# Graph network kernel: 127-partition gathers and a separate gather for the last partition in one sum stage

## What is computed

```python
def _hypergraph_conv(x, node_idx, edge_idx, D_inv, B_inv, W, b):
    xt = x @ W
    e = B_inv[:, None] * jax.ops.segment_sum(xt[node_idx], edge_idx, num_segments=NUM_HYPEREDGES)
    out = D_inv[:, None] * jax.ops.segment_sum(e[edge_idx], node_idx, num_segments=NUM_NODES)
    return out + b
...
h = jax.nn.relu(_hypergraph_conv(x, node_idx, edge_idx, D_inv, B_inv, W1, b1))
y = _hypergraph_conv(h, node_idx, edge_idx, D_inv, B_inv, W2, b2)
```

## Time and profile before

| | us |
|---|---|
| Median of 3 runs | 21875.0 |
| Lowest, highest | 21866.0, 21877.35 |
| Profiled execution, span from first to last instruction | 16599.4 |
| Profiled execution, its own total | not given apart from its span |
| POOL busy in the span | 11914.9 |
| DVE busy in the span | 10015.7 |
| The stage "conv1s", first gather to the end of the last | 2077.0 |

### The profile page before, as it was taken

How to read it: one execution, slowest core, us unless ns; L and a number is a source line. 1 busy time by engine, 2 the same in 40 slices (tenths; PEclk the granted TensorE clock), 3 DMA queues, 4 the chain that set the end, 5 groups by cost and what they waited for, 6 DMA issues and landing times. The chain is left out here.

```text
span 16599.4 us, 101583 instructions
## 1 busy us (share of the span) xinstructions
PE 4027.8 (24%) x22758; PEld 3127.6 (19%) x22758; DVE 10015.7 (60%) x17532; ACT 4595.6 (28%) x4609; POOL 11914.9 (72%) x12292
## 2 busy tenths in 40 slices
PE   2333356667311111111111222222111111100000
PEld 1222246666311000000000122222100000000000
DVE  7777787777573333322222477777566666576776
ACT  1111122222102222223333255554011111244342
POOL 6777757777627777767777677776777776777775
PEclk7555578888755555555555555555555555555555
DMA  2222222222262222212222234433233332344443
GB/s 85 64 60 59 59 79 80 77 78 80 102 241 55 59 59 64 60 50 64 59 60 59 74 125 133 133 125 112 63 84 84 84 84 73 118 150 156 154 152 103
DMA packets 564633, 1517.57 MB, mean 91 GB/s; under 512 B 270008, under 2 KB 270541, under 8 KB 516610
## 3 DMA queue, kind: packets, MB, share of 16 engines
q1 hardware_dynamic: 169982, 1028.88, 16.6%
q0 software_dynamic: 392160, 467.91, 12.9%
q10 hardware_dynamic: 2068, 16.12, 0.2%
HBM read 714.46 MB, written 803.57 MB: 91 GB/s over the span
## 5 line engine op out<-in xcount | busy, mean ns | idle before, releaser
L926 POOL DMA_INDIRECT rows<-tab,idx x6656 | 6444.0, 968 | 2118.2 <-issue 2027.2
L572 POOL DMA_INDIRECT moved_rows<-recs,sidx x1664 | 1687.3, 1014 | 570.7 <-issue 506.3
L926 POOL DMA_INDIRECT rows<-in_x,idx x1664 | 1588.4, 955 | 512.8 <-issue 506.8
L926 POOL DMA_INDIRECT rows<-sums,idx x1664 | 1570.2, 944 | 511.8 <-issue 506.8
L1351 DVE TENSOR_TENSOR_SCAN FB<-mask,FB 128x1430 f32<-128x1430 f32 x156 | 463.7, 3027 | 1837.1 <-ACT FB L1324 1837.1
L989 PE MATMUL dist_ps<-dist_w,a3T 65*128 65x512 f32 x416 | 392.7, 1100 | 3937.5 <-ACT a3T L1013 3920.7
L989 PEld LDWEIGHTS dist_ps<-dist_w,a3T 65*128 65x128 f32 x416 | 122.1, 324 | 4078.3 <-issue 3882.8
L1049 DVE TENSOR_REDUCE small<-SQ 128x16 f32<-128x1024 f32 x104 | 127.5, 1226 | 1083.4 <-ACT SQ L1032 726.9
L1773 PE MATMUL lg<-bd_fcr,attrT 128*128 128x128 f32 x1664 | 401.3, 422 | 1529.4 <-ACT attrT L1793 1529.4
L1324 ACT ACTIVATE FB<-rows 128x4096 f32<-128x4096 f32 x52 | 371.2, 7138 | 1349.3 <-DMA rows<-tab,idx 755.0
L1773 PEld LDWEIGHTS lg<-bd_fcr,attrT 128*128 128x128 f32 x1664 | 361.4, 321 | 1572.9 <-ACT attrT L1793 1572.8
(11 more groups left out here) (462 smaller groups left out, 19370.0 us busy)
## 6 DMA issues: line engine op xcount, KB each, us to landing
rows<-tab,idx POOLq DMA_INDIRECT x6656
sums<-DN SPq DMA_DIRECT2D x64, 1664.0 KB, 6.6
sums<-DN SPq DMA_DIRECT2D x32, 3328.0 KB, 10.8
spread<-zeros SPq DMA_DIRECT2D x52, 1040.0 KB
own<-spread SPq DMA_DIRECT2D x26, 2080.0 KB
sums<-rows SPq DMA_DIRECT2D x26, 2048.0 KB
dists<-Y SPq DMA_DIRECT2D x104, 512.0 KB, 2.7
recs<-sums SPq DMA_DIRECT2D x26, 2048.0 KB
```

The source lines that it names most:

```text
L572: pool.indirect_dma_start(moved_rows if fill else rec, bass.IndirectOffsetOnAxis(ap=idx[b][:, j:j + 1], axis=0), recs[b][:, j, :], None).t ...
L926: pool.indirect_dma_start(rows[b][:, j, :], None, table, bass.IndirectOffsetOnAxis(ap=idx[b][:, j:j + 1], axis=0)).then_inc(rows_in[b], 16)
```

## The change

In the stage "conv1s" alone, by a new argument `apart`. The 64 gathers of a chunk now cover partitions 0 to 126. The 64 rows of partition 127 in a chunk come by one more gather, issued on POOL ahead of the 64: it fetches 64 rows into 64 partitions of a small buffer `tail` (row `j` into partition `j`), by indices that SP has loaded into `tail_idx`. SP then stores `tail` into a DRAM buffer `tail_rows` (64 rows of 64 floats in a row), waits for it, and loads these 4096 floats into partition 127 of `rows`. ACT waits for this load besides the 64 gathers. POOL waits in addition for the tail's indices and for the tail's buffer. What is computed stays as it was.

```diff
@@ -1253,11 +1253,14 @@
                     dve.tensor_copy(last[:, F:F + 1], last_n[:, :]).then_inc(carried, 1)
 
 
+    tail_rows = dram("tail_rows", [2, T, F])
+
     @phase
-    def sum_flat(name, o, idx_arr, table, to, last, first, mean=False):
+    def sum_flat(name, o, idx_arr, table, to, last, first, mean=False, apart=False):
 
 
         TB, FM = T + 1, 22
+        PG = P - 1 if apart else P
         thirds = [(f, min(f + FM, F)) for f in range(0, F, FM)]
         S = lambda n: [sem(f"{name}_{n}{b}") for b in range(2)]
         q = lambda n: sem(f"{name}_{n}")
@@ -1274,6 +1277,11 @@
             FB_flat, mask_flat = FB.rearrange("p f t -> p (f t)"), mask.rearrange("p f t -> p (f t)")
             sums_by_edge = FB[:, :, 1:TB].rearrange("p f t -> p t f")
             dist = Distances(c, name, first, 1, pa, gains, ss)
+            if apart:
+                tail_idx_in, tail_in, tail_out, tail_back = S("tail_idx"), S("tail_rows"), S("tail_out"), S("tail_back")
+                tail_idx = [alloc(c, f"tail_idx{b}", [T, 1], I32) for b in range(2)]
+                tail = [alloc(c, f"tail{b}", [T, F]) for b in range(2)]
+                tail_ids = idx_arr.rearrange("(p t) -> p t", p=P)[P - 1]
 
             @block.sync
             def _(sp):
@@ -1281,9 +1289,22 @@
                     if not isinstance(i, int) or i:
                         sp.wait_ge(rows_in[b], i * 16 * T)
                     sp.dma_start(idx[b][:, :], cols(idx_arr, i * 2 + b)).then_inc(idx_in[b], 16)
+                    if apart:
+                        if not isinstance(i, int) or i:
+                            sp.wait_ge(tail_in[b], i * 16)
+                        ids = tail_ids[bass.ds((i * 2 + b) * T, T)]
+                        sp.dma_start(tail_idx[b][:, :], ids.rearrange("(t a) -> t a", a=1)).then_inc(tail_idx_in[b], 16)
                     dist.load(sp, i, b, 0)
                     if not isinstance(i, int) or i or b:
                         store(*((i - 1, 1) if b == 0 else (i, 0)))
+                    if apart:
+                        move_tail(i, b)
+
+                def move_tail(i, b):
+                    sp.wait_ge(tail_in[b], i * 16 + 16)
+                    sp.dma_start(tail_rows[b], tail[b][:, :]).then_inc(tail_out[b], 16)
+                    sp.wait_ge(tail_out[b], i * 16 + 16)
+                    sp.dma_start(rows[b][P - 1:P, :, :], tail_rows[b:b + 1]).then_inc(tail_back[b], 16)
 
                 def store(i, b):
                     dist.store(sp, i, b, 0)
@@ -1296,7 +1317,22 @@
 
             @block.gpsimd
             def _(pool):
-                gathers(pool, table, idx, rows, idx_in, rows_in, lambda e, i, b: e.wait_ge(taken, i * 2 + b - 1), go, T, NCH)
+                if apart:
+                    def gather(i, b):
+                        if not isinstance(i, int) or i:
+                            pool.wait_ge(taken, i * 2 + b - 1)
+                            pool.wait_ge(tail_out[b], i * 16)
+                        pool.wait_ge(tail_idx_in[b], (i + 1) * 16)
+                        pool.wait_ge(idx_in[b], (i + 1) * 16)
+                        pool.sem_inc(go, 1)
+                        pool.indirect_dma_start(tail[b][:, :], None, table,
+                                                bass.IndirectOffsetOnAxis(ap=tail_idx[b][:, 0:1], axis=0)).then_inc(tail_in[b], 16)
+                        for j in range(T):
+                            pool.indirect_dma_start(rows[b][0:PG, j, :], None, table,
+                                                    bass.IndirectOffsetOnAxis(ap=idx[b][0:PG, j:j + 1], axis=0)).then_inc(rows_in[b], 16)
+                    pairs(pool, gather, NCH)
+                else:
+                    gathers(pool, table, idx, rows, idx_in, rows_in, lambda e, i, b: e.wait_ge(taken, i * 2 + b - 1), go, T, NCH)
 
             @block.tensor
             def _(pe):
@@ -1318,6 +1354,8 @@
                     k = keep[o][:, bass.ds(ch * T, T)].unsqueeze(1).to_broadcast([P, FM, T])
                     act.activation(mask[:, :, 1:TB], k, ACT.Copy).then_inc(masked, 1)
                     act.wait_ge(rows_in[b], (i + 1) * 16 * T)
+                    if apart:
+                        act.wait_ge(tail_back[b], (i + 1) * 16)
                     act.wait_ge(carried, ch + 1)
                     if not first:
                         act.wait_ge(out_made, ch)
@@ -2417,7 +2455,7 @@
         last = alloc(c, "last", [P, F + 1])
         sum_flat("conv1d", "d", src_in, tab, sums, last, 1, mean=True)
         carry("conv1d", "d", sums, last, None, mean=True)
-        sum_flat("conv1s", "s", sedge, sums, sums_s, last, 2)
+        sum_flat("conv1s", "s", sedge, sums, sums_s, last, 2, apart=True)
         carry("conv1s", "s", sums_s, last, None)
         A = alloc(c, "A", [P, NJ, F])
```

## The result

| | before | after |
|---|---|---|
| Median | 21870.96 us (4 runs, 21866.0 to 21877.35) | 25167.39 us (4 runs, 25158.76 to 25191.18) |
| Ratio | | 1.1511, 95% interval 1.1497 to 1.1524 |
| Span of the profiled execution | 16599.4 us | 25163.8 us |

The change costs 3296 us, 15%. The forecast was 21617 us in a range of 21310 to 23100; the sign and the range are both missed.

A forecast was written before the change was run, and what follows sets the result against it. The prediction took POOL's making of gathers to bound the changed stage. It summed -262 us for cheaper gathers including the tail's, +1 us for waits and +3 us for start and end to 21617 us, range 21310 to 23100.

The forecast's parts named there:

- What bounds the kernel: Stage conv1s: POOL's making of gathers bounds it, 79.9 us a chunk; ACT's loop sets a floor of 58.4 us.
- Part 1: POOL, head of each chunk: 26 added tail gathers at the full price of 1.249 us, +32.5 us.
- Part 2: POOL's 1664 gathers: 127 partitions cut each from 0.944 to 0.766 us, -262 us including the added tail gathers.
- Part 3: Queue 0: a gather on one DMA engine takes 2.7 us, delaying only the landing, +2.5 us once at the stage's end.
- Part 4: SP's added loads, store and waits for the tail fit within POOL's chunk and cost nothing.
- Part 5: Start and end of the stage: a second small index load and the late landing add +3 us.
- Rival A: POOL's gathers: the price stays at 944 ns, 21911.5 us in all; chance 0.18.
- Rival B: POOL's gathers: one engine's list costs more, 23039 us at 1.62 us a gather, 22339 us at 1.2; chance 0.32.
- C: Gathers: always the same single DMA engine bounds each at 2.70 us, 24327 us in all; chance 0.05.
- D: Gathers fall under 0.588 us and ACT's loop bounds the stage, 21320 us; chance 0.45 together with the forecast.

The follow-up runs named there:

- e2: The changed kernel with its 64 gathers back at 128 partitions and the tail's load sent to an unread tile: 21908.07 us beside 21877.05, ratio 1.0014.
- e3: The changed kernel without the tail's gather and SP's steps for it, gathers still of 127 partitions: 25132.19 us beside 21877.05, ratio 1.1487.
- e1: The kernel before, unedited, traced a second time: 21880.62 us, span 21878.9 us.
- e4: As e3, with eight gathers a chunk each of 128, 126, 120, 125, 124, 122, 121 and 127 partitions: 22414.79 us beside 21877.05.
- e5: As e3, with eight gathers a chunk each of 113, 61, 31, 16, 64, 96, 118 and 112 partitions: 17363.17 us beside 16601.05.
- e7: As e3, with all 64 gathers of a chunk covering 124 partitions: 17285.11 us beside 16601.05.
- e9: As e3, with each gather of 127 partitions split into one of 112 and one of 15: 18635.49 us beside 16601.05.
- e11: As e3, with each column gathered twice, 128 gathers a chunk, all of 16 partitions: the stage takes 3875.7 us.

## Why the prediction was wrong, point by point

- *What bounds the kernel.* Right for the trace that it was read from and for the changed kernel, where ACT waits for gathers in all 26 chunks, and the loss is the gathers' alone (e2, e3). For the timed runs of the kernel before it is wrong: there ACT waits once, 17.1 us, and a chunk takes ACT 92.0 us and not 58.4 (e1). So cheaper gathers could hardly have brought the -262 us in those runs; that is an argument from e1's trace, and no run had cheaper gathers there. That the 5275.6 us around the span stay as they are was a wrong reading: they don't lie around the span but within it, in executions of the long setting (e1), and some of them lie in this stage.
- *Part 1, one more gather a chunk.* Right where POOL is the bound: expected +32.5 us with a full price of 0.944; the tail's gather takes 916 ns, and 26 with their gaps take 31.7 us of what the change has over e3. That e2 has +31 us in all is partly luck, by what e1 shows of the bound.
- *Part 2, the 127 partitions.* Wrong, and this is the step that failed. The sentence was "I take the middle of what can still gain, (0.944 + 0.588)/2 = 0.766 us", with the reason that "the lists that hold data fall from 16 to 1". The number of lists doesn't set the price, and their length does: 13.2 ns a step, and with 127 steps instead of 8 a gather takes 2550 ns where it took 944. The part had taken 178 ns off the price, and 1606 ns came on. The argument from the earlier trace rows, that the price doesn't follow the bytes, holds, and says nothing on entries, since 256 B rows and 512 B rows make as many of them. Of the Trainium skill's sentences in "DMA: Bandwidth & Descriptors", the rule of the largest divisor, 1 for 127 partitions, is what the packets show for an indirect gather too, and the exception for direct copies is not; that all 16 engines report agrees with the sixteen closing packets of 4 B, and the 15 without rows get 127 fillers each besides. And a second term was missing: the pauses, 937.5 us in the stage, which the part put at nothing because no row of the kernel before has one.
- *Part 3, DMA time.* The rows do go to one engine. Their packets take 2.06 us a gather (2.70 expected), under the 2.85 us from one gather to the next. Queue 0's share rose from 13.5% to 28.1% over 2.7 times the time, mostly by fillers. That the landing costs only its delay once, at the end, holds between the pauses; in the pauses POOL goes on only behind the last packet.
- *Part 4, SP.* Right, within about a microsecond. SP's steps of one chunk after the change, with ACT's copy and PE's transpose:

```profile
13015.74 0.92 POOL L1328 DMA_INDIRECT tail<-sums,tail_idx  x1 [0.30 <-issue]
...
13018.98 7.14 ACT L1362 ACTIVATE FB<-rows 128x4096 f32<-128x4096 f32 x1 [158.64 <-DMA rows<-sums,idx]
...
13042.90 0.36 SPq L1312 DMA_DIRECT2D sums_s<-OUT  x1
...
13043.37 0.48 SPq L1305 DMA_DIRECT2D tail_rows<-tail  x1
...
13052.90 0.26 SPq L1307 DMA_DIRECT2D rows<-tail_rows  x1
13053.37 0.42 SPq L1291 DMA_DIRECT2D idx<-sedge  x1
...
13055.62 1.33 SPq L974 DMA_DIRECT2D a<-attr_d  x1
...
13067.30 0.42 PE L984 MATMUL pa<-ident,a 128*128 128x128 f32 x1
```

The tail's load goes out 10.0 us behind the store of the sums (9.6 expected), the index load 10.5 us behind it (10 expected), and PE takes the distance input 11.7 us behind its load at line 974. ACT's copy waits for the gathers and not for any of it.
- *Part 5.* The 3 us are too few to be told apart in any run here.
- *Rival A* (price stays): out. The remark of the Trainium skill ("DMA: Bandwidth & Descriptors", "Anatomy of one DMA") that the making of descriptors adds little until there are many fits lists of up to 8 steps fairly well (842 ns at 1 step, 948 at 8), and not lists of 127, where making them is most of the 2550 ns.
- *Rival B* (a longer list costs more): this is what happened, with the mechanism as it was put: "128 rows in 16 lists take under 1 us in all, as if the 16 were written side by side, 8 steps deep; one list would be 127 steps deep". It was given 0.32, below the forecast's 0.45, and 1.62 us a gather instead of 2.55; that price was of a held-up gather and had nothing to do with steps. The far end of 2.70 us was nearer and was left out of the range, but it is the time of a DMA engine, and that it lies near 2.55 is chance. Even with 2.55 B would have given 64 x 2.855 + 1.25 = 184.0 us a chunk and 24585 us. The pauses, which no rival had, add 863 us, and the bound read from the other setting takes some 250 us off again (247 us in e1); what is left is within 35 us of the 25167 measured.
- *Rivals C and D*: out. C's sum of 24327 us is the nearest on record to what was measured, but by luck: one engine has the rows, as C has it, and doesn't hold POOL up, since its packets take 2.06 us a gather and begin after POOL has ended it. D is out because the gathers didn't get cheaper.

The sum by measured terms, in the short setting, where nothing else disturbs the stage: 2673.8 us for 1664 gathers (4244.0 - 1570.2), 31.7 us for 26 tails with their gaps, 863.4 us for 234 pauses (934.8 less 0.305 each), together 3568.9 us; the stage grew by 5646.1 - 2077.0 = 3569.1 us.

No run here beats the kernel before. A gather of 16 rows, the fewest measured, still takes 0.84 + 0.3 us. So fewer gathers would be needed, and no run here has a form that fetches more rows with one.

## What to carry to other kernels

Give a gather on POOL a count of rows that is a multiple of 16, or at least has a divisor near it (121 and 120 rows cost 1.0 us): leaving out one partition of 128 cost 2.7 times the price. Where the count can't be had, two gathers can be cheaper than one: 112 + 15 rows beat 127, though the 15 had other rows' indices. When a count changes, look at what it divides by before its size, and let the price of a form that the trace doesn't have be bounded by the worst mechanism that is consistent with the rows, not by the row that looks nearest. And set a trace's span against the timed runs first: one that is a quarter shorter is of another execution, and neither its idle times nor the bound read from them are those of the runs.

## What the runs showed of the hardware

- A gather on POOL takes 0.83 to 0.87 us plus 13.2 ns for each step of its longest list, measured at sixteen counts from 16 to 128 rows, with lists of 1 to 127 (e4, e5).
- The rows of a gather go to as many DMA engines as the largest divisor of their count up to 16, by the packet sizes of the same sixteen counts. The engines that get no rows get fillers, so that their lists are as long: 144 packets for 127 rows, 32 for 128.
- POOL pauses for 2.5 to 4.5 us where the lists would reach 1024 entries, and also behind 128 gathers, counted from the last pause or the chunk's begin (e3 to e7, e9 to e11). It goes on 0.9 to 2.4 us after the last packet of queue 0. In the changed kernel the pauses are a quarter of the loss, 863 of 3569 us.
- The same program runs in 16600 us or in 21870 us. Within a set of timed runs it was always one of the two, but the first trace is of the short setting beside timed runs of the long one. In the long setting idle time called "issue" grows, in the whole program from 19.1 to 8943.7 us on PE, 35.5 to 2749.5 on DVE and 84.7 to 4243.2 on ACT, and hardly on POOL (3778.6 to 4064.3). The changed stage, bound by POOL, takes 5648.1 and 5646.1 us in the two. The cause is open.
